# Joining the last two groups of key gates at both Gelus, with their values made three batches sooner, in a two-layer transformer kernel

## What is computed

```python
logits = jnp.einsum('bqhd,bkhd->bhqk', Q, K) * scale
attn = jax.nn.softmax(jnp.where(causal, logits, -jnp.inf), axis=-1)
h = x @ dp_w1 + dp_b1                      # 64 features of each token
h = (h - mu) / jnp.sqrt(var + LN_EPS) * ln_g + ln_b
drift = (_gelu(h) @ dp_w2 + dp_b2)[..., 0]
g = _gelu(drift[..., None] * g_w1[0] + g_b1)    # 16 features
gate = jnp.tanh(g @ g_w2 + g_b2)[..., 0]
gated = attn * gate[:, None, None, :]
out = jnp.einsum('bhqk,bkhd->bqhd', gated, V).reshape(B, S, E)
```

## Time and profile before

| | |
|---|---|
| median of 3 runs | 961.76 us (960.02 to 963.63) |
| the profiled execution | 962.33 us, its span 960.6 us |
| PE busy | 900.8 us, 94% of the span |
| DVE busy | 700.0 us, 73% |
| ACT busy | 634.9 us, 66% |
| POOL busy | 367.0 us, 38% |
| the chain of work that ended last | PE 68%, DVE 21%, ACT 5%, issue 3%, DMA 2% |

### The profile page before, as it was taken

How to read it: one execution, slowest core, us unless ns; L and a number is a source line. 1 busy time by engine, 2 the same in 40 slices (tenths; PEclk the granted TensorE clock), 3 DMA queues, 4 the chain that set the end, 5 groups by cost and what they waited for, 6 DMA issues and landing times.

```text
span 960.6 us, 17779 instructions
## 1 busy us (share of the span) xinstructions
PE 900.8 (94%) x6420; PEld 638.7 (66%) x6420; DVE 700.0 (73%) x1889; ACT 634.9 (66%) x1103; POOL 367.0 (38%) x439
## 2 busy tenths in 40 slices
PE   4598998989999999999999999999999999999996
PEld 3354554545567888777777777776777566999982
DVE  7986787886579968686877878687885865643664
ACT  6477778776687766667767777777777566654420
POOL 4365145140001101242545517255361515268881
PEclk9687999999999999999999999999999999999999
DMA  5845343654042125210211111110111513022327
GB/s 132 236 127 137 95 125 104 184 152 128 16 133 63 37 54 139 68 42 26 67 44 45 45 45 45 44 66 23 56 55 27 173 45 110 26 71 81 87 71 241
DMA packets 86179, 83.15 MB, mean 87 GB/s; under 512 B 8978, under 2 KB 72456, under 8 KB 86092
## 3 DMA queue, kind: packets, MB, share of 16 engines
q1 hardware_dynamic: 80868, 73.33, 26.9%
q0 software_dynamic: 4320, 8.27, 2.6%
q10 hardware_dynamic: 904, 0.42, 0.1%
HBM read 50.54 MB, written 31.72 MB: 86 GB/s over the span
## 4 chain that ended last, share of the span: by engine, by line
PE 68%; DVE 21%; ACT 5%; issue 3%; DMA 2%; SPq 1%; POOL 0%; POOLq 0%; DVEq 0%; ACTq 0%
PE psum L1582 18%; PE psum L1624 10%; PE psum L1605 6%; PE psum L1619 6%; PE psum L1420 4%; DVE pieces L2121 3%; PE psum L1359 3%; DVE maxes L1998 3%; PE psum L1402 2%; PE psum L1539 1%; PE psum L1375 1%; PE psum L1329 1%; PE psum L1496 1%; DVE tmp L2186 1%; DVE gb_tok L2136 1%
## 5 line engine op out<-in xcount | busy, mean ns | idle before, releaser
L1582 PE MATMUL psum<-parts,q_stack 128*128 128x512 f32 x640 | 250.3, 472 | 1.7 <-DVE parts L2318 1.0
L2620 ACT ACTIVATE big<-psum,cols 128x512 f32<-128x512 f32 x205 | 140.1, 688 | 75.3 <-PE psum L1582 72.9
L2848 POOL TENSOR_TENSOR hT<-hT,gb_tok 128x512 f32<-128x512 f32 x54 | 75.9, 1405 | 265.2 <-DVE gb_tok L2136 264.2
L1582 PEld LDWEIGHTS psum<-parts,q_stack 128*128 128x128 f32 x640 | 111.7, 190 | 52.9 <-issue 39.5
L1998 DVE TENSOR_REDUCE maxes<-psum 128x4 f32<-128x1024 f32 (+1 forms) x96 | 114.5, 1216 | 28.9 <-PE psum L1375 28.4
L1582 PE MATMUL psum<-parts,k_stack 128*128 128x512 f32 x320 | 126.1, 394 | 0.0
L1624 PE MATMUL psum<-big,ew 128*128 128x512 f32 x232 | 118.4, 593 | 0.0
L1619 PE MATMUL psum<-pieces,w_parts 128*128 128x512 f32 x336 | 97.8, 399 | 0.0
L2928 POOL DMA_INDIRECT routed<-big,slot_i x64 | 65.5, 1023 | 52.6 <-DVE slot_i L2305 31.1
L2121 DVE TENSOR_TENSOR pieces<-big,pieces 128x512 fp32r<-128x512 f32 x89 | 76.2, 862 | 10.9 <-ACT pieces L2627 10.9
L2951 POOL DMA_INDIRECT answers<-hT,to x64 | 62.6, 979 | 34.5 <-DVE hT L2333 19.2
(11 more groups left out here) (432 smaller groups left out, 1889.7 us busy)
## 6 DMA issues: line engine op xcount, KB each, us to landing
gb_tok<-gate_rows SPq DMA_DIRECT2D x32, 512.0 KB, 3.7
q_stack<-q_pieces SPq DMA_DIRECT2D x32, 192.0 KB, 3.4
...
```

Source lines behind the costliest of these rows:

```text
L1582: last = eng.matmul(bank(i), w1_part(wp, e)[:, fs], parts[2 * xk + xp][:, :], start=n == 0, stop=n == 2)
L2620: eng.activation(slots[held("slot", "up", n, e, f)], bank(held("bank", "up", n, e, f)), ACT.Relu, bias=col("L0_ffn_b1", e * FC + f)).then_ ...
L2848: eng.tensor_tensor(hT[:, ns], xpT[:, ns] if e == 0 else hT[:, ns], gate_wide[:, e // GHELD % 2, e % GHELD, :], ALU.add).then_inc(sem("acc ...
```

## The change

Groups 2 and 3 go through the two Gelus as one: `gv_g` runs once for both, after `gv_a 2` and `gv_a 3`, and `gv_h` once for both, after `gv_d 2` and `gv_d 3`. `gv_w`, `gv_d`, `gv_r`, `gv_t` and `gv_v` remain two steps each, now behind the joint one. For batches 12 to 15 `normalise` and `val` get a rank 180 lower, which is three batches sooner. Groups 0 and 1 are left as they are. Everything after the first of these steps is planned anew, so the order moves on all engines.

```diff
+GELUS = ((0,), (1,), (2, 3))
...
+def gelu_group(n):
+
+    return next(group for group in GELUS if n in group)
...
-        normalise(0, 0, b, 60 * (b - 4) + 4, pool="early")
+        normalise(0, 0, b, 60 * (b - 4 - (3 if b >= 12 else 0)) + 4, pool="early")
...
-               rank=60 * (b - 3) + 4,
+               rank=60 * (b - 3 - (3 if b >= 12 else 0)) + 4,
...
+    gate_tiles = [p.buffer("early") for _ in range(NT // GT)]
...
-        p.step("gv_g", n, work="act:3.2", urgent=4 if n else 8, after=[("gv_a", n)], tmp=tile)
-        p.step("gv_w", n, work="pool:1.3", urgent=4 if n else 8, after=[("gv_g", n)], tmp=tile)
+        if n == gelu_group(n)[-1]:
+            p.step("gv_g", n, work=f"act:{2.56 + .64 * len(gelu_group(n))}", urgent=4 if n else 8, after=[("gv_a", m) for m in gelu_group(n)], tmp=tile)
+    for n in range(NT // GT):
+        tile, last = gate_tiles[n], gelu_group(n)[-1]
+        p.step("gv_w", n, work="pool:1.3", urgent=4 if n else 8, after=[("gv_g", last)], tmp=tile)
...
-        p.step("gv_h", n, work="act:2.9", urgent=4 if n else 8, after=[("gv_d", n)], tmp=tile)
-        p.step("gv_r", n, work="dve:.55", urgent=4 if n else 8, after=[("gv_h", n)], closes=[(0, tile)], tmp=tile)
+        if n == last:
+            p.step("gv_h", n, work=f"act:{2.56 + .34 * len(gelu_group(n))}", urgent=4 if n else 8, after=[("gv_d", m) for m in gelu_group(n)], tmp=tile)
...
             def gv_g(n):
-                t = T(held("tmp", "gv_g", n))[:, :]
-                w.wait_ge(*done("gv_a", n))
-                eng.activation(t, t, ACT.Gelu).then_inc(sem("gv_g"), 1)
+                for m in gelu_group(n):
+                    t = T(held("tmp", "gv_q", m))[:, :]
+                    w.wait_ge(*done("gv_a", m))
+                    last = eng.activation(t, t, ACT.Gelu)
+                last.then_inc(sem("gv_g"), 1)
```

More of the change, by code:

```diff
@@ L465, in order_steps @@
                 p.step("write", n, w, h, work=f"{write_queue(n, w, h)}:1.5 dma:2.2", urgent=3 if n == 0 else 0, after=[pieces_done(n, w)])
+    gate_tiles = [p.buffer("early") for _ in range(NT // GT)]
     for n in range(NT // GT):
-        tile = p.buffer("early")
+        tile = gate_tiles[n]
         p.step("gv_q", n, work="act:.63", urgent=2 if n else 12, after=[("val", b) for b in range(n * GT // TPB, (n + 1) * GT // TPB)],
@@ L471, in order_steps @@
         p.step("gv_a", n, work="pool:3.7", urgent=4 if n else 8, after=[("gv_s", n), ("rows",)], tmp=tile)
-        p.step("gv_g", n, work="act:3.2", urgent=4 if n else 8, after=[("gv_a", n)], tmp=tile)
-        p.step("gv_w", n, work="pool:1.3", urgent=4 if n else 8, after=[("gv_g", n)], tmp=tile)
-        p.step("gv_d", n, work="dve:1.5", urgent=4 if n else 8, after=[("gv_w", n)], tmp=tile)
-        p.step("gv_h", n, work="act:2.9", urgent=4 if n else 8, after=[("gv_d", n)], tmp=tile)
-        p.step("gv_r", n, work="dve:.55", urgent=4 if n else 8, after=[("gv_h", n)], closes=[(0, tile)], tmp=tile)
+        if n == gelu_group(n)[-1]:
[3 more added lines that the diff above has]
+        p.step("gv_w", n, work="pool:1.3", urgent=4 if n else 8, after=[("gv_g", last)], tmp=tile)
+        p.step("gv_d", n, work="dve:1.5", urgent=4 if n else 8, after=[("gv_w", n)], tmp=tile)
+        if n == last:
+            p.step("gv_h", n, work=f"act:{2.56 + .34 * len(gelu_group(n))}", urgent=4 if n else 8, after=[("gv_d", m) for m in gelu_group(n)], tmp=tile)
+    for n in range(NT // GT):
+        tile, last = gate_tiles[n], gelu_group(n)[-1]
+        p.step("gv_r", n, work="dve:.55", urgent=4 if n else 8, after=[("gv_h", last)], closes=[(0, tile)], tmp=tile)
         p.step("gv_t", n, work="act:.35", urgent=4 if n else 8, after=[("gv_r", n)])
@@ L1985, in gv_r @@
                 g3 = T(held("tmp", "gv_r", n))[:, 0:GT * GW].rearrange("p (t n) -> p t n", n=GW)
-                w.wait_ge(*done("gv_h", n))
+                w.wait_ge(*done("gv_h", gelu_group(n)[-1]))
                 eng.tensor_tensor(g3, g3, row("L0_attn_g_w2").unsqueeze(1).to_broadcast([P, GT, GW]),
@@ L2482, in gv_g @@
             def gv_g(n):
-                t = T(held("tmp", "gv_g", n))[:, :]
-                w.wait_ge(*done("gv_a", n))
-                eng.activation(t, t, ACT.Gelu).then_inc(sem("gv_g"), 1)
-            def gv_h(n):
-                t = T(held("tmp", "gv_h", n))[:, 0:GT * GW]
-                w.wait_ge(*done("gv_d", n))
-                eng.activation(t, t, ACT.Gelu).then_inc(sem("gv_h"), 1)
+                for m in gelu_group(n):
[3 more added lines that the diff above has]
+                last.then_inc(sem("gv_g"), 1)
+            def gv_h(n):
+                for m in gelu_group(n):
+                    t = T(held("tmp", "gv_q", m))[:, 0:GT * GW]
+                    w.wait_ge(*done("gv_d", m))
+                    last = eng.activation(t, t, ACT.Gelu)
+                last.then_inc(sem("gv_h"), 1)
             def gv_t(n):
@@ L2818, in gv_w @@
                 t3 = T(held("tmp", "gv_w", n))[:, :].rearrange("p (t n) -> p t n", n=HID)
-                w.wait_ge(*done("gv_g", n))
+                w.wait_ge(*done("gv_g", gelu_group(n)[-1]))
                 eng.tensor_tensor(t3, t3, row("L0_attn_dp_w2").unsqueeze(1).to_broadcast([P, GT, HID]),
```

## The result

The changed kernel takes 965.75 us (median of 16 runs, 962.73 to 966.69) beside 961.25 us of the kernel before in the same session (16 runs, 958.89 to 963.63): a ratio of 1.0038 [1.0029, 1.0047], slower by 3.7 us (4.5 between the medians), within the 0.5% that I had set as no change. I had said 967.5, with 956 to 975 as the range; the time lies in it, though in the band that I had given 0.31, and not in the one of a clear slowdown, which had 0.52. Its profiled execution took 966.11 us with a span of 964.3 us, against 962.33 and 960.6 before.

A forecast was written before the change was run, and what follows sets the result against it. PE was taken as the bound. A stall of 11.8, 0.4 at `mrow 9` and a wait of 3.4, less 10.2 taken away, gave 5.4 us more: 967.5 us, range 956 to 975.

The forecast's parts named there:

- PE is the bound, and a saved microsecond of ACT counts only where PE waits: In the attention stage and behind it PE is nearly always busy, while ACT, which saves 7.7 us of loads, has idle time.
- Taken away, 10.2 us: PE's gaps at groups 2 and 3, 6.2 us, the 2.4 us wait for `mrow 12` and 1.6 us of slow clock go.
- The stall ahead of `pv 8 0`, 11.8 us: PE waits for group 2's gates until V + 23.6, with 11.8 us of work meanwhile; V is PE's end of `val 15`.
- The upper bound, 13.3: Largest stall at `pv 8 0`, from group 3's earlier gate time of 20.5 us plus a second `gv_w` and `gv_d`.
- `mrow 9`, 0.4: Ahead of the stall, `mrow 9` follows `max 9 5` by less PE work than a maximum takes: 0.4 us more.
- The wait at `max 12 0`, 3.4 us: PE waits for `stack 12`, queued on SP behind `bg 0` and `bg 1`; PE there at V + 30.9, data at V + 34.3.
- Nothing given back behind it: Maxima of batches 10 and 11, done early, free DVE later where PE hardly waits for it: costed at nothing.
- the third rival: Gaps from 222 to 275.8 us vanish (2.5 us), the `max 12 0` wait halves (1.7): 963.3, no change; chance 0.19.
- moved work of 1.5 us: `ln_t` of batches 2 and 3 and some `po_*` go ahead of the first `up`; comes back behind, costed at nothing.
- the gates sooner (955.0): At `pv 8 0` the gates come sooner than DVE's queue says, stall 3 us, no `max 12 0` wait: 955.0; chance 0.14.
- A clock that stays low or a collision with `bg 2`: Clock low beyond `max 12 0`, and `mrow 12` or `stack 13` meets `bg 2` or `bg 3`: 973.5; chance 0.14.
- The loads in full (954.1): Each of ACT's six saved table loads is on the path, so 7.7 us go: 954.1; chance 0.07.

The follow-up runs named there:

- e10: The kernel before with Square in place of Gelu in both steps of groups 2 and 3 (result wrong): 958.29 us, 0.9974 times before.
- e8: The changed kernel with POOL's `rest 7 1` and the cuts behind it waiting for DVE's `gv_d 3`: 990.48 us, 1.0090 times before, on a slower chip.
- e3: The changed kernel with weight loads `bg 0` and `bg 1` put behind `stack 12` on SP's queue: 963.85 us, 1.0027 times before.
- e9: The changed kernel run once more, unaltered: 965.74 us, 1.0048 times before.
- e2: The changed kernel with the ranks of batches 12 to 15 as in the kernel before, so joining alone: 969.41 us, 1.0085 times before.
- e7: The kernel of e4 with `bg 0` to `bg 3` held behind `mrow 10` to `mrow 13`: 977.30 us, 0.9945 times before, on a slower chip.
- e11: The kernel of e7 again, beside the changed kernel on the same chip: 956.40 us, 0.9954 times before.
- e4: The changed kernel with values of batches 12 to 15 six batches sooner instead of three, those of 8 to 11 three sooner: 969.05 us, 1.0077 times before.

## Why the prediction held, step by step

- *PE is the bound, and a saved microsecond of ACT counts only where PE waits*: right. In e10 10.3 us of ACT brought 2.5 (1.2 to 3.9); in after 6.2 us less of ACT came with 3.7 us more.
- *Taken away, 10.2 us*: all the gaps and the slow clock of the earlier trace rows are gone in after. (They are eleven, four and six and one; I called the last the seventh.) That I took the most rather than 6.2 was right here. As the effect of the loads it is wrong: by e10 three of group 2's gaps don't come of them, so they went because the work was planned anew.
- *The stall ahead of `pv 8 0`, 11.8 us*: right in place and cause, too small. I had it end at V + 23.6 (my own terms, with three handovers of 0.1, give 23.4); `pv 8 0` starts at V + 27.9, so the term is 27.9 - 11.8 = 16.1. `gv_s 3` took the 2.4 us and the twelve maxima 13.8 instead of 13.6. `gv_d 2` took 2.3 us more (the port, e8), and `gv_r 2` was done at V + 23.0 instead of 20.5. Group 2's values were ready at about V + 26.2. The rest is PE's: `po_w`, `po_x` and `po_t` stand between `mrow 11` and `pv 8 0`, and they ran at a clock of 0.50. I had PE's 11.8 us of work at the whole clock; the clock was 0.73 in the mean over the stretch, and the work took 15.1. I had priced the slow clock only behind the stall; it lay inside it. The idle time itself, 12.8 us, is within 1 of my 11.8. The upper bound, 13.3, was too low, since it held neither.
- *`mrow 9`, 0.4*: 0.3.
- *The wait at `max 12 0`, 3.4 us*: 2.3, and e3 shows cause and price (1.1 to 1.9 us at the end, not clear of noise). PE came later than I had it, at V + 36.1.
- *Nothing given back behind it*: wrong, and this is part of what balances the stall. Idle time from 222 us to the first `up` fell from 2.5 to 1.35 us, and the half clock that lay at 245 us for 3.4 us (1.7 us of work) didn't return: 2.9 us. That was part of the third rival, whose 2.5 came near by luck: of the idle time only 1.15 us went, and the clock it hadn't counted. It had misread the gaps too; they are 0.55, 1.41 and 0.44 us, not half a microsecond each. Its other half, a wait of 1.7 us less at `max 12 0`, was 1.1.
- *The sum*: 16.1 + 0.3 + 2.3 - 10.2 - 2.9 = 5.6, beside 5.4 predicted and 3.7 to 4.5 measured. With the moved work of 1.5 us the first `up` should be 7.1 us late; it is 5.6. PE's own total says more: from 134.8 us to the first `up` it is idle for 17.1 us instead of 11.8 and busy for 128.6 instead of 128.3. So the 5.6 us are idle time; the lower clock cancels (3.3 us inside the stall, 1.6 and 1.7 gone elsewhere), and of the 1.5 us of moved work hardly any shows. In e9, the same kernel, it is 16.4 and 130.7, so what I can't place, 1.5 us, is no more than two executions differ by. The mechanism was right, but that the number came out within 2 us is luck: a stall 4.3 us too small stood against 2.9 us given back and a wait 1.1 us too long.
- *The other rivals*: the gates sooner (955.0) needs a stall under 6.4 us; with the gates' chain at 26.8 to 27.9 us in after, e2 and e8 alike, that takes room ahead of `pv 8 0`, which e7 and e11 gave it. A clock that stays low or a collision with `bg 2`: not in after, but e4 shows that mechanism at 13.2 us. The loads in full (954.1): refuted by e10.
- *What the profile would show*: two loads, DVE busy, the gap at `max 12 0`, none at `exp 12 0`: right. PE idle 12 us in 24: 12.8 in 28. First `up` 7 us later: 5.6.
